# Expert 0's tokens chosen in two halves, the first beside the last batch

## The reference, cut to what matters

```python
# x: 8 x 512 tokens of 512 channels = 4096 tokens
y = einsum(x * styles, weight) * dcoefs            # per batch b of 8
y = clip(y + bias, -256, 256)
scores = softmax(y.reshape(4096, 512) @ Wr)        # 8 experts
G, idx = top_k(scores.T, 1024)                     # each expert takes its best 1024 tokens
h   = gelu(y[idx] @ W1 + b1)                       # 512 -> 2048
X_e = h @ W2 + b2                                  # 2048 -> 512
out = x + scatter_add(idx, G * X_e)
```

## Time and profile before

| | |
|---|---|
| median of three runs | 1477.13 us (1476.48 to 1478.94) |
| the profiled execution | 1476.48 us |
| its span | 1474.7 us |
| TensorE busy | 1456.0 us (99%) |
| VectorE busy | 957.5 us (65%) |
| ScalarE busy | 727.8 us (49%) |
| GpSimd busy | 406.1 us (28%) |
| mean granted clock of TensorE | 0.992 |

### The profile page before, as it was taken

One profiled execution on the slowest core, in us unless ns is written; L12 is line 12 of the kernel. 1 busy time (PEld: TensorE's weight loads), 2 busy tenths in 40 slices (PEclk: granted clock), 3 DMA queues, 4 the chain that ended last, 5 costly groups with the idle time before them and its releaser, 6 DMA issues.

```text
span 1474.7 us, 18730 instructions
## 1 busy us (share of the span) xinstructions
PE 1456.0 (99%) x6557; PEld 1196.5 (81%) x6557; DVE 957.5 (65%) x1630; ACT 727.8 (49%) x992; POOL 406.1 (28%) x379
## 2 busy tenths in 40 slices
PE   9996999999999999999999999999999999999998
PEld 7785888888888888888888888888888888888887
DVE  6676777577557764677556864777556764777543
ACT  6774554564445443554446444554445443554442
POOL 1002202432224522353233522352223422030003
PEclk9997999999999999999999999999999999999999
DMA  7966684874273642754255633663174625351114
GB/s 241 251 186 153 165 293 133 200 107 90 36 153 63 136 58 61 140 88 92 44 143 72 122 57 94 108 120 74 38 151 64 128 44 122 94 116 57 51 43 57
DMA packets 168972, 163.83 MB, mean 111 GB/s; under 512 B 111776, under 2 KB 112544, under 8 KB 167856
## 3 DMA queue, kind: packets, MB, share of 16 engines
q1 hardware_dynamic: 147568, 120.20, 37.8%
q0 software_dynamic: 21168, 42.44, 13.7%
q10 hardware_dynamic: 144, 0.01, 0.0%
HBM read 113.16 MB, written 33.77 MB: 100 GB/s over the span
## 4 chain that ended last, share of the span: by engine, by line
PE 96%; DVE 1%; DMA 1%; SPq 0%; issue 0%; ACT 0%; POOL 0%; DVEq 0%; ACTq 0%
PE Pt L1992 21%; PE BBt L1992 20%; PE BBt L1932 18%; PE Pt L1932 18%; PE BBt L1921 6%; PE Pt L1876 6%; PE BBt L1675 5%; PE Pt L1717 1%; PE BBt L2003 1%; DMA XB<-in_xT 1%; PE Pt L1890 0%; PE BBt L1905 0%; DVE OB L1227 0%; PE Pt L1733 0%; DMA XR<-y_rows,idx 0%
## 5 line engine op out<-in xcount | busy, mean ns | idle before, releaser
L635 POOL DMA_INDIRECT slots<-VS,slot x192 | 202.5, 1055 | 457.4 <-DVE BBt L1481 145.1
L1992 PE MATMUL Pt<-RG 128*128 128x512 f32 x1176 | 283.6, 389 | 0.0
L1992 PE MATMUL BBt<-RG 128*128 128x512 f32 x1170 | 281.8, 390 | 0.0
L1932 PE MATMUL BBt<-XT,RG 128*128 128x512 f32 x1176 | 280.3, 389 | 0.0
L1932 PE MATMUL Pt<-XT,RG 128*128 128x512 f32 x1176 | 279.1, 389 | 0.0
L1932 PEld LDWEIGHTS BBt<-XT,RG 128*128 128x128 f32 x1176 | 220.5, 188 | 46.2
L1992 PEld LDWEIGHTS Pt<-RG 128*128 128x128 f32 x1176 | 220.4, 188 | 46.2
L1932 PEld LDWEIGHTS Pt<-XT,RG 128*128 128x128 f32 x1176 | 220.7, 188 | 45.8
L1992 PEld LDWEIGHTS BBt<-RG 128*128 128x128 f32 x1170 | 219.1, 188 | 47.6 <-issue 2.3
L933 ACT ACTIVATE RG<-RAW 128x512 fp32r<-128x512 f32 x98 | 61.8, 631 | 228.5 <-PE BBt L1992 228.5
L1493 DVE TENSOR_TENSOR RG<-RAW,RG 128x512 fp32r<-128x512 f32 x98 | 67.9, 693 | 163.7 <-ACT RG L933 163.7
(11 more groups left out here) (308 smaller groups left out, 1775.4 us busy)
## 6 DMA issues: line engine op xcount, KB each, us to landing
RAW<-in_W SPq DMA_DIRECT2D x224, 256.0 KB, 4.6
W1R<-in_W SPq DMA_DIRECT2D x32, 256.0 KB, 3.8
W2R<-in_W SPq DMA_DIRECT2D x32, 256.0 KB, 4.5
y_rows<-XR SPq DMA_DIRECT2D x32, 256.0 KB, 2.6
XB<-in_xT SPq DMA_DIRECT2D x7, 1024.0 KB, 6.8
slots<-VS,slot POOLq DMA_INDIRECT x192
B<-in_b SPq DMA_DIRECT2D x8, 256.0 KB, 7.4
WTraw<-in_WT SPq DMA_DIRECT2D x4, 256.0 KB, 5.3
```

Source lines behind the costliest of these rows:

```text
L635: eng.indirect_dma_start(tab_d[e - 2][:, :], bass.IndirectOffsetOnAxis(slot[:, t, e:e + 1], 0), VS[:, t, e, :], None, bounds_check=K - 1, ...
L1932: last = mm((Pt, BBt)[g % 2][:, bank, :], wslot(g)[:, a, w, 128 * k:128 * k + 128], XT[:, b, d, k, :], start=(begins and k == 0 and m == 0 ...
L1992: last = mm((Pt, BBt)[t // 4][:, t % 4, :], hslot(j)[:, a, hcol(t):hcol(t) + 128], wk(jj)[:, d, :], start=(j == 0 and m == 0), stop=(j == ...
```

## The change

Expert 0's 1024 tokens are found in two searches of 512. The first takes the best 512 of the first 28 tiles (seven batches). It runs while TensorE does batch 7: the matmuls of batch 7 are issued between the rounds. The second search looks in all 32 tiles without those chosen, in iterations 0 to 9 of expert 0. Both have ten rounds of three bits and no histogram.

- TensorE: router(6) comes after cond(7, 0), router_t(1) within cond(7, 1); logits(c) goes to bank 0 chunk by chunk. `total` and `rank` stand in `search` and `search_late`; `lists0(1)` after iteration 8. Of 13 `busy_rows` five are left.
- POOL: clips batch 7 and makes its low halves. It gathers rows 0 to 3 once batch 6 is stored, rows 4 to 7 after the second list; the copies of x to out start after A(0) instead of A(7).
- VectorE: the tables move from the start to behind batch 1 (`tables`). The search for seven experts picks by a scan from TAB2, without the four `cnext` instructions.
- ScalarE: xm_hi(7) for all chunks earlier, the load of the Gelu table after the last exp.
- SP: batch 7's rows go through a buffer of their own (XR7). The transposes of tiles 4 to 7 are at SP's i = 13 and 14, their unpacking at iterations 12 to 14 instead of 6 to 13.

```diff
 # tensor
+            b = NB - 1
+            cond(b, 0, (0, 1, 2, 3))
+            router(b - 1)
+            cond(b, 1, (0, 1))
+            router_t(1)
+            cond(b, 1, (2, 3))
+            cond(b, 2, (0,))
+            replicate(0)
+            for r in range(1, 11):
+                total(0, r, lambda: cond(b, 2 + r // 4, (r % 4,)) if r < 8 else logits(r - 8) if r < 10 else None)
+            rank(0)
+            logits(2)
+            logits(3)
...
+            def total(k, r, filler=None):
+                pc = ((IB, AB[0])[r % 2] if k == 0 else TB)[:, 0:8]
+                if k == 0:
+                    mm(pc, OS[:, :], KC0[:, :], start=True, stop=False)
+                if filler:
+                    filler()
+                eng.wait_ge(s_cnt0, 11 * k + r + 1)
+                if k:
+                    mm(pc, OS[:, :], KC0[:, :], start=True, stop=False)
+                mm(pc, cnt0[:, 0:1].broadcast_to([128, 128]), E8[:, :], start=False, stop=True).then_inc(s_pc0, 1)
...
-            busy_rows(9)
-            count(0)
+            busy_rows(2)
+            replicate(1)
+            to_rows()
+            busy_rows(2)
+            turn(0)
+            total(1, 1)
             busy_rows(1)
-            turn(0)
-            busy_rows(2)
             turn(1)
-            busy_rows(1)
+            total(1, 2)
             A_pair(0, 0)
...
+                if i in (2, 3, 4, 5):
+                    total(1, 2 * i - 1 if i > 2 else 4)
+                if i == 6:
+                    rank(1)
...
+            def search_late(i):
+                if i == 2:
+                    count(1)
+                if i in (3, 4, 5):
+                    total(1, 2 * i)
+                if i == 8:
+                    for q in range(4):
+                        lists0(1, q)
 # gpsimd
+            b = NB - 1
+            for c in range(4):
+                eng.wait_ge(s_ce, 4 * b + c + 1)
+                yv = YT[b % 2][:, c, :]
+                eng.tensor_scalar(yv, yv, -CLAMP, CLAMP, ALU.max, ALU.min).then_inc(s_cl, 1)
+                eng.wait_ge(s_yh, 4 * b + c + 1)
+                eng.tensor_tensor(YL[:, c, :], yv, asf(YH[:, c, :]), ALU.subtract).then_inc(s_yl, 1)
 # vector
+            def compare(k, r, scores):
+                now = first[:, 0:1].bitcast(f32) if r == 1 else TH[:, 7:8]
+                eng.tensor_scalar(junk, scores, now, None, ALU.is_ge, ALU.add,
+                                  accum_out=cnt0[:, 0:1]).then_inc(s_cnt0, 1)
+                eng.tensor_tensor(CN, now.bitcast(i32).broadcast_to([128, 8]), XT8[:, r - 1, :],
+                                  ALU.bitwise_xor).then_inc(s_v, 1)
+                chain[0] += 1
+            def settle(k, r):
+                eng.wait_ge(s_pc0, 11 * k + r + 1)
+                eng.wait_ge(s_v, chain[0])
+                sums = (IB, AB[0])[r % 2] if k == 0 else TB
+                link(eng.tensor_tensor_scan(TH, CNf, sums[:, 0:8], 0.0, ALU.max, ALU.min))
...
+            def second_list(i, late):
+                if (i, late) in ((0, 1), (2, 1), (3, 0), (3, 1), (4, 0), (4, 1), (5, 0)):
+                    r = {(0, 1): 3, (2, 1): 4, (3, 0): 5, (3, 1): 6, (4, 0): 7, (4, 1): 8, (5, 0): 9}[(i, late)]
+                    settle(1, r)
+                    compare(1, r + 1, RB)
+                if (i, late) == (5, 1):
+                    settle(1, 10)
+                    masks()
+                if (i, late) == (6, 0):
+                    ranks0(1)
+                if (i, late) == (6, 1):
+                    rows0(1)
+                if (i, late) == (7, 1):
+                    onehot0(1, 0)
+                    onehot0(1, 1)
+                if (i, late) == (8, 0):
+                    onehot0(1, 2)
+                    onehot0(1, 3)
+                if (i, late) == (9, 0):
+                    numbers0(1)
```

More of the change, by code:

```diff
@@ L668, in _ @@
             eng.wait_ge(s_idx, 1)
-            for c in range(8):
+            for c in range(4):
                 if c == 3:
@@ L785, in _ @@
             eng.wait_ge(s_c["bias"], 16)
-            for b in range(NB):
+            for b in range(NB - 1):
                 evac(b, 0)
@@ L1196, in _ @@
-                if b == 5:
-                    at_least(0, s_v)
-                    chain[0] += 1
-                    counted()
+                lower(b, 0)
+                lower(b, 1)
+                if b == 1:
+                    tables()
+            lower(NB - 2, 2)
+            lower(NB - 2, 3)
+            eng.memset(zero, 0.0)
+            softmax(1)
+            eng.wait_ge(s_cnt0, 1)
+            eng.tensor_copy(S0[:, 0:NT - 4], SR[:, 0:NT - 4, 0])
+            CNf = CN.bitcast(f32)
@@ new lines, in onehot0, with numbers0 @@
+            def onehot0(k, q):
+                n = 8 if k or q < 3 else 4
+                eng.tensor_tensor(OHT[:, q, :, 0:n], slb[:, None, 8 * q:8 * q + n].broadcast_to([128, 128, n]),
+                                  iot[:, :, 0:n], ALU.is_equal).then_inc(s_oh, 1)
+            def numbers0(k):
+                eng.wait_ge(s_im, 4 * k + 4)
+                v = (TB if k else IB)[:, 0:8].rearrange("p (v h) -> p h v", v=2)
+                with nc.allow_low_precision(reason="token numbers below 4096 are exact"):
+                    eng.tensor_reduce(idx[:, 0, 4 * k:4 * k + 4], v, AX.X, ALU.add).then_inc(s_idx, 1)
@@ L1265, in count @@
                 last.then_inc(s_cnt, 1)
-                for k in range(4):
-                    last = eng.tensor_scalar(cnext[:, :, k], cand[:, :], k * (step >> 2), None, ALU.bitwise_or)
-                last.then_inc(s_v, 1)
-                chain[0] += 1
             def select(n):
                 eng.wait_ge(s_pc, n + 1)
-                eng.wait_ge(s_v, chain[0])
-                link(eng.tensor_tensor(cnextf[:, 1:4, :], (IB, TB)[n % 2][:, 0:3, None].broadcast_to([128, 3, 4]),
-                                       cnextf[:, 1:4, :], ALU.min))
@@ L1542, in _ @@
             w1_lo(1)
-            prepare()
-            count(0)
+            eng.wait_ge(s_pc0, 12)
+            link(eng.tensor_copy(RB, TB[:, 0:256]))
             row_lower(0)
+            compare(1, 1, RB)
             row_lower(1)
+            settle(1, 1)
+            compare(1, 2, RB)
             turned_lo(0)
@@ L1549, in _ @@
             turned_lo(1)
+            eng.wait_ge(s_s2t, 1)
+            eng.tensor_copy(S2[:, :], AB[1][:, 0:256]).then_inc(s_s2c, 1)
             row_lower(3)
-            select(0)
             turned_lo(2)
+            settle(1, 2)
+            compare(1, 3, RB)
             turned_lo(3)
-            count(1)
+            eng.wait_ge(s_s2c, 1)
+            count(0)
+            def second_list(i, late):
[5 more added lines that the diff above has]
+                    settle(1, 10)
+                    masks()
+                if (i, late) == (6, 0):
[10 more added lines that the diff above has]
+                    numbers0(1)
             for i in range(NBLK):
@@ L2006, in last_tile @@
                     last.then_inc(s_yt, 1)
+            def search_late(i):
[4 more added lines that the diff above has]
+                if i == 8:
+                    for q in range(4):
+                        lists0(1, q)
             for q in range(4):
-                lists(0, q)
-            to_rows()
+                lists0(0, q)
             def busy_rows(n):
@@ L2035, in _ @@
             A_pair(1, 2)
-            count(1)
+            total(1, 3)
+            count(0)
             for i in range(2, NBLK + 1):
@@ L2041, in _ @@
                 if i == 22:
-                    all_lists(1)
+                    for q in range(4):
+                        lists(q)
                 if i == NBLK:
```

531 lines of the change are left out of this document (249 added, 282 removed).

## The result

| | before | after |
|---|---|---|
| median | 1476.91 us (1475.34 to 1478.94, 16 runs) | 1480.36 us (1477.73 to 1482.9, 16 runs) |
| ratio | | 1.0022, 95% interval 1.0015 to 1.0029 |
| span of the profiled execution | 1474.7 us | 1478.0 us |
| granted clock, mean | 0.992 | 0.991 |

The forecast was 1472.0 with a range to 1476.5; the kernel became 3.5 us slower, the side that the prediction gave 9 in 100.

What follows compares the result with a forecast made beforehand. TensorE, busy 1456 of 1474.7 us, was taken as the bound. 1.35 + 7.85 + 0.4 - 0.9 - 0.6 - 2.1 - 0.7 = 5.3 us off 1476.48 gave 1471.2, as a median 1472.0; range 1468.4 to 1476.5.

Steps and rivals of the forecast that it cites:

- The x blocks and copies of x move, without a new deadline that binds: Expert 0's iterations behind A(2): moving these transfers was costed at nothing, since A(16) is two iterations off.
- Tables off the start, 1.35: Kernel start: without VectorE's small table instructions, the matmuls after cond0(3) begin at 22.65 instead of 24.01, gaining 1.35 us.
- Threshold, 7.85, near 122.5: Search beside batch 7: ten rounds end at 123.9 instead of 131.75, 7.85 us gained; near 122.5 with the earlier start.
- Threshold to token numbers, 0.4 less: Ranks and lists after the search: 0.4 us less, from 28 tiles and 4 columns instead of 32 and 8.
- Gathers among the stores, 0.9: Row gathers meeting SP's last transposes and stores of batch 7: 0.9 us lost (0 to 2.5).
- Rival 2: Gathers queue behind transposes and stores and TensorE starts the expert cold: 1.6 + 1.9 us more, 1475.5 us; chance 0.13.
- Clock, 0.6: After the last filler the clock falls, rising near A_pair(0, 0) with some half-width matmuls slow: 0.6 us lost (0 to 2.5).
- Behind A(2), 2.1 and 0.7: Second search in expert 0's iterations: 2.1 us of added TensorE work, 0.7 (0 to 2) from a late count on VectorE.
- Rival 4: VectorE's queue sets the pace in iterations 2 to 9, every microsecond per iteration costing 8: slower, 1480.1 us; chance 0.08.

Runs made afterwards that it cites:

- x_copies_clear: Changed kernel with the copies of x after A(5), A(7), A(13), A(15), the last two also behind the transposes of rows 4 to 7: 1475.7 us, 0.9981 of the kernel before.
- x_three_logits: Changed kernel, x copies clear, batch 7's transposes and stores behind W1 loads, its clips on VectorE, its logits(2), (3) behind the first list: 1475.45 us, 0.9992.
- x_clear_stores: As x_copies_clear, with SP's transposes and stores of batch 7 issued behind the loads of W1(3) and W1(4): 1474.05 us, 0.9969 of the kernel before.
- x_three_warm: As x_clear_stores, with batch 7's clips on VectorE and 16 more unread matmuls from search round 8 to turn(2): 1472.18 us, 0.9971 of the kernel before.
- x_tables_alone: Kernel before the change with only VectorE's small table instructions moved from the start to behind batch 1: ratio 0.9992, not to be told from none.
- x_before_early: Kernel before the change with only the copies of x moved ahead, after A(0), A(2), A(4) and A(6): ratio 1.0173, 27 us slower.
- x_late_copies: Changed kernel with the copies of x at their old places, after A(7), A(9), A(11), A(13): 0.9999; seven of twelve executions 1475.5 to 1476.4 us, five 1494 to 1513.

## Why the prediction was wrong

**The step that failed** is the last sentence of the change part by part: "The x blocks and copies of x move, without a new deadline that binds". I asked only when the copies are needed, and not what they meet. Their deadline is indeed far away. But four copies of 2 MB each, started at A(0) to A(6), stood beside loads of 256 KB that the next iterations wait for: 15 us instead of 3.7 for a load, TensorE idle from 164.5 to 167.8, and half clock for some 4 us after. The term was 0 and measured 4.4 to 6; without it the sign would have been right (x_copies_clear, 0.9981), though not the size: the forecast was 0.9965. The profile of before had a hint of it: from 184 to 188, where the first copy runs, the DMA engines are busy for 1.04 of the time at 367 GB/s, beside 0.14 in the four microseconds ahead of it.

The Trainium skill, DMA: Bandwidth & Descriptors, Queues, rings and completion order, says that each DMA engine takes turns between the queues that have work for it, a whole packet at a time. That a load from one queue slows down when another is full agrees with the 3.7 and 15 us; no run here shows the turns themselves.

**Point by point**, the rest of the sum, by x_copies_clear where the copies are out of the way:

- *Tables off the start, 1.35.* 1.30 at clock 1.00. In another execution a fall of the clock took it all back.
- *Threshold, 7.85, near 122.5.* 122.7 to 123.3, and in the changed kernel 7.7 of the 7.85, once the earlier start is taken off (8.66 less 0.94). It came out near because two errors cancel. The ten rounds took 12.0 us, not 11.3: the low halves cost 2.0, where the prediction put both together at 1.3 (its own parts, three times 0.4 and three times 0.1, make 1.5). In turn the first compare came 0.2 us sooner than the 111.3 forecast, though the start had given 0.9 of its 1.35. The length of the low half was right (1.28 for 1.2), that of the clip wrong (1.92 for 0.6), but the clips cost CN nothing instead of 0.1 each: the lock shows here between CN and an instruction of two inputs alone, though the clip too reads SBUF. The Trainium skill, GPSIMD Engine Reference, Elementwise — side-by-side cycle accounting, gives 1.8 cycles an element as the best case of a tight loop, an estimated 0.77 us for 512 at 1.2 GHz; the clip, with two operations, took two and a half times that.
- *Threshold to token numbers, 0.4 less.* Nothing: 5.85 us as before. The logits of batch 7, at half clock 1.00 us for four, stand ahead of the list. x_three_logits gave the 0.4 back and lost more.
- *Gathers among the stores, 0.9.* 2.4 in the changed kernel (10.7 against 8.3) and 2.9 in x_copies_clear, at and above the upper end of what I allowed. Rival 2 was right in this part of its mechanism; x_clear_stores takes 2.3 of the 2.9 away.
- *Clock, 0.6.* 0.5 to 1.5: from the unpacking of the last row to A(2) are 6.2 us in the kernel before, 6.7 in the changed one and 7.7 in x_copies_clear. A_pair(0, 0) alone took 1.2 longer, and the fillers of x_three_warm gave 1.6 back at the end.
- *Behind A(2), 2.1 and 0.7.* 3.9 (82.3 from A(2) to A(16), 78.4 before). The second list's 32 matmuls took 2.10 us, and A(8) with them 7.6 instead of 5.6: 2.0 for the 0.8 of the sum. The prediction took the wrong row for it. The list of the earlier trace rows belongs to another expert and has its one-hot weights side by side; expert 0's own list in the kernel before reads them with a stride, as both new lists do, and took nearly as long per matmul at clock 0.50 as the second list at 1.00:

```profile
135.30 2.26 PE L1857 MATMUL Pt<-RH,OH 128*128 128x16 bf16 x32 [2.82 <-DVE OH L1357]
...
192.28 2.10 PE L1912 MATMUL Pt<-RH,OH 128*128 128x8 bf16 x32
```

In the iterations VectorE's queue was no pace: 5.6 to 5.9 us, but for A(3), 6.4. Rival 4, the one that ended on the slower side, did not happen; the time came out where it ends, for another reason.

Trace against trace, the terms give 4.6 at A(2) and 0.7 at A(16), while the medians of x_copies_clear and the kernel before differ by 2.7. The likely rest is the kernel before, whose profiled execution was quick in this place. In x_tables_alone and x_before_early, which are the same there, ScalarE idled 3.1 us from 146.7 on, and A(2) came at 154.0 instead of 152.1, with the rows landing at the same time. What it waited for isn't in the trace and stays open. So the gain up to A(2) and the clock's cost, both read against the quick execution, are uncertain by some 2 us.

## What to carry to other kernels

A transfer that is moved is judged by what it runs beside, not by its own deadline: list the loads in flight in its new place and how many microseconds their buffers cover, and how far it is from the next transfer of its kind. A bulk copy is put where no DMA transpose is in flight, and where the loads beside it can be late. Where TensorE has to wait anyway, matmuls without a use just before the work resumes brought the whole gain that could be told here; those at the start of the wait added none to it. And a cost is taken from the row with the same operands: two of the terms were priced from a row that was only nearby.

## What was not expected of the hardware

- A DMA transpose on SP's queue beside 2 MB copies issued by GpSimd: 29.50 and 10.82 us in x_before_early, against 1.24 to 1.27 alone. The executions of x_late_copies, in which the two may meet, fall in two groups, 18 to 37 us apart.
- Loads of 256 KB landed in 14.5 to 16.6 us beside copies issued 4 to 11 us apart, of which two were in flight for a part of the time (the changed kernel, 150 to 157 us). They took 4.3 to 7.4 beside a single one and 3.4 to 3.7 without (medians).
- GpSimd's clip of 128 x 512 fp32 with two operations took 1.92 to 2.05 us, longer than its subtraction with two inputs (1.27 to 1.30). The subtraction held VectorE's xor of two SBUF inputs until its own end each time it had begun first; the clip never did (0.16 to 0.18 us beside it in all five traces that have it).
- 32 one-hot matmuls of 8 columns whose weights are read with a stride took 2.10 us at clock 1.00, twice the 0.97 of 32 with 40 columns and contiguous weights. With the stride the clock made no difference: 28 of them took 1.86 at 0.50. The stride as cause wasn't tried by itself.
- The granted clock fell to 0.50 just behind 20 us, with TensorE busy throughout, in one of the fourteen profiled executions (x_tables_alone); in the other thirteen it is 1.00 there.
